# A transformer kernel on one core: transposes moved to the projection banks and row sums moved to VectorE in the cross-attention stages

## The reference

```python
# layer 0: x = x + Attn(LN(x), LN(ctx)) ; x = x + MLP(LN(x))
# layer 1: x = x + SelfAttn(LN(x)) ; x = x + CrossAttn(LN(x), ctx) ; x = x + MLP(LN(x))
xn = layernorm(x, ln1_w, ln1_b)                       # 512 tokens x 512
q = (xn @ Wq).reshape(B, N1, H, hd).transpose(0, 2, 1, 3)   # H = 16 heads of 32
k = kv[:, :, 0].transpose(0, 2, 1, 3)                 # 77 keys for each of the 8 batches
attn = softmax(einsum('bhqd,bhkd->bhqk', q, k) * scale, axis=-1)
o = einsum('bhqk,bhkd->bhqd', attn, v).transpose(0, 2, 1, 3).reshape(B, N1, C1)
x = x + (o @ Wproj + bproj)
```

## Time and profile before

| what | value |
|---|---|
| median of 3 runs | 3474.11 us (3473.83 to 3480.76) |
| the profiled execution's own time | 3480.76 us |
| its span | 3479.0 us |
| PE busy | 3188.6 us, 92% of the span |
| DVE, ACT, POOL busy | 1764.3, 1631.5, 1332.3 us (51, 47, 38%) |
| TensorE's clock as granted, mean | 0.956 of full |
| first cross-attention stage | about 105 to 526 us |
| second cross-attention stage | about 2317 to 2741 us |

### The profile page before, as it was taken

How to read it: one execution, slowest core, us unless ns; L and a number is a source line. 1 busy time by engine, 2 the same in 40 slices (tenths; PEclk the granted TensorE clock), 3 DMA queues, 4 the chain that set the end, 5 groups by cost and what they waited for, 6 DMA issues and landing times. The chain is left out here.

```text
span 3479.0 us, 42311 instructions
## 1 busy us (share of the span) xinstructions
PE 3188.6 (92%) x14480; PEld 2521.0 (72%) x14480; DVE 1764.3 (51%) x2720; ACT 1631.5 (47%) x3492; POOL 1332.3 (38%) x1355
## 2 busy tenths in 40 slices
PE   6599997999999958999999999958999799999999
PEld 5478876888888845666766766636787588888887
DVE  4477754323233225777777777746776442222221
ACT  2376653322222214666666666626777332222222
POOL 0354431333333323666666665644544211111110
PEclk8799998999999978999999999979999899999999
DMA  4422313211111122343343334332222321110000
GB/s 136 119 64 75 88 55 118 70 49 49 49 49 49 49 97 70 92 117 104 101 114 109 103 97 109 99 94 61 82 73 69 106 91 37 37 37 30 30 28 35
DMA packets 215049, 264.36 MB, mean 76 GB/s; under 512 B 78460, under 2 KB 100580, under 8 KB 214836
## 3 DMA queue, kind: packets, MB, share of 16 engines
q1 hardware_dynamic: 214835, 261.66, 25.4%
HBM read 125.12 MB, written 60.42 MB: 53 GB/s over the span
## 5 line engine op out<-in xcount | busy, mean ns | idle before, releaser
L1065 DVE TENSOR_REDUCE L1sa_nmax<-L1sa_s 128x2 f32<-128x1024 f32 x256 | 310.7, 1214 | 213.9 <-PE L1sa_s L884 213.9
L1157 POOL TENSOR_TENSOR L1sa_El<-L1sa_E,L1sa_Eh 128x1024 fp32r<-128x1024 f32 x128 | 320.7, 2506 | 150.4 <-ACT L1sa_Eh L972 131.1
L468 DVE TENSOR_TENSOR L1ff_gl<-L1ff_gf,L1ff_gh 128x512 fp32r<-128x512 f32 x128 | 95.8, 748 | 473.8 <-ACT L1ff_gh L428 473.8
L468 DVE TENSOR_TENSOR L0ff_gl<-L0ff_gf,L0ff_gh 128x512 fp32r<-128x512 f32 x128 | 99.1, 774 | 437.9 <-ACT L0ff_gh L428 437.9
L414 ACT ACTIVATE L1ff_gf<-L1ff_f,cols 128x512 f32<-128x512 f32 x128 | 88.3, 690 | 450.7 <-PE L1ff_f L94 450.7
L414 ACT ACTIVATE L0ff_gf<-L0ff_f,cols 128x512 f32<-128x512 f32 x128 | 88.3, 690 | 450.3 <-PE L0ff_f L94 450.3
L981 ACT ACTIVATE L1sa_E<-L1sa_st 128x1024 f32<-128x1024 f32 x256 | 260.5, 1017 | 48.1 <-PE L1sa_st L896 47.9
L92 PE MATMUL L1ff_f<-L1ff_hTh,L1ff_Wh 128*128 128x512 f32 x512 | 203.3, 397 | 5.7 <-POOL L1ff_hTl L235 5.7
L92 PE MATMUL L0ff_f<-L0ff_hTh,L0ff_Wh 128*128 128x512 f32 x512 | 203.1, 397 | 5.7 <-POOL L0ff_hTl L235 5.7
L972 ACT ACTIVATE L1sa_Eh<-L1sa_E 128x1024 fp32r<-128x1024 f32 x192 | 200.7, 1045 | 0.2
L94 PE MATMUL L1ff_f<-L1ff_hTl,L1ff_Wh 128*128 128x512 f32 x512 | 200.4, 391 | 0.0
(11 more groups left out here) (284 smaller groups left out, 8648.7 us busy)
## 6 DMA issues: line engine op xcount, KB each, us to landing
L1sa_OLN<-L1sa_osb SPq DMA_DIRECT2D x128, 192.0 KB, 2.7
L0ff_xs<-x SPq DMA_DIRECT2D x64, 256.0 KB, 3.0
L1sa_stack_q<-L1sa_parts_q SPq DMA_DIRECT2D x128, 128.0 KB, 2.6
L1sa_stack_k<-L1sa_parts_k SPq DMA_DIRECT2D x128, 128.0 KB, 2.6
L1ff_xs<-x SPq DMA_DIRECT2D x64, 256.0 KB, 3.4
L0ca_xs<-in_x SPq DMA_DIRECT2D x32, 256.0 KB, 3.0
L0ca_stage<-in_x SPq DMA_DIRECT2D x32, 256.0 KB, 2.8
x<-L0ca_stage SPq DMA_DIRECT2D x32, 256.0 KB, 2.0
```

Of the source, the lines that this page charges most:

```text
L468: nc.vector.tensor_tensor(gl[:, j % 2, :], gf[:, j % 2, :], f32(gh[:, j % 2, :]), ALU.subtract)\
L1065: nc.vector.reduce_max(nmax[:, h % 2, 2 * (n % 2):2 * (n % 2) + 2], s_bank[:, :, :], AX.X, negate=True)\
L1157: nc.gpsimd.tensor_tensor(El[:, n % 2, :], E[:, n % 3, :], f32(Eh[:, n % 2, :]), ALU.subtract)\
```

## The change

The `T` transposes become units like `Q` and `O`: they take the `pj` banks in the common turn and stand in `CA_ORDER` behind the last query projection of the batch; their own halves (`T_HALVES`) and their own turn (`turn_bank`) go, and the `t` banks hold probabilities alone. The 36 pieces of a batch (32 before) are dealt out over the 24 halves. DVE sums all tiles, so no exponential has an accumulator. `BIAS` moves to halves 1, 8, 13 and 17. ACT, DVE and POOL take a `T` unit in the half behind the one in which it ends.

```diff
-CA_ORDER = [("Q", 0, 3), ("O", -1, 0), ("O", -1, 1), ("Q", 1, 0), ("O", -1, 2), ("Q", 1, 1), ("O", -1, 3), ("Q", 1, 2)]
-CA_FIRST = [("Q", 0, g) for g in range(3)]
-
-T_HALVES = (3, 4, 5, 6)
+CA_ORDER = ([("Q", 0, 3)] + [("T", 1, c) for c in range(KT)]
+            + [("O", -1, 0), ("Q", 1, 0), ("O", -1, 1), ("Q", 1, 1), ("O", -1, 2), ("O", -1, 3), ("Q", 1, 2)])
+CA_FIRST = [("T", 0, c) for c in range(KT)] + [("Q", 0, g) for g in range(3)]
...
-    quarters = [(*u, c) for u in CA_ORDER for c in range(KT)]
+    quarters = [(*u, c) for u in CA_ORDER for c in range(1 if u[0] == "T" else KT)]
...
-        SUM_BY = ("act", "dve", "act", "dve")
+        SUM_BY = ("dve", "dve", "dve", "dve")
         LAST_TILE = (B - 1, 3 * (TILES - LEAD) // 2)
-        STATS, NORMS, BIAS = (13, 14, 15, 16), (19, 20, 21, 22), (1, 3, 9, 14)
+        STATS, NORMS, BIAS = (13, 14, 15, 16), (19, 20, 21, 22), (1, 8, 13, 17)
...
             def bank_free(u):
                 kind, b, i = units[u - 2]
-                if kind == "Q":
+                if kind == "T":
+                    pe.wait_ge(x.e_hf.sem, x.e_hf.at(b, i))
+                elif kind == "Q":
                     pe.wait_ge(e_ql.sem, e_ql.at(b, i))
...
                 if c == 0 and u >= 2:
                     bank_free(u)
-                if kind == "Q":
+                if kind == "T":
+                    if i == 0:
+                        pe.wait_ge(x.e_xn.sem, x.e_xn.at(b, TT - 1))
+                    ln_transpose(nc, x, bank, i, cst.ident[:, :]).then_inc(x.e_tr.sem, x.e_tr.unit)
+                elif kind == "Q":
...
-                bank = turn_bank("P", b, v)
+                if b * CA_STEPS + v >= 2:
+                    pe.wait_ge(e_pl.sem, e_pl.no(b * CA_STEPS + v - 2))
...
             def evacuate(kind, b, i):
-                if kind == "Q":
+                if kind == "T":
+                    whole(b, i)
+                elif kind == "Q":
                     q_hi(b, i)
...
-                    if half - 1 in T_HALVES and exists(b + 1):
-                        hi(b + 1, T_HALVES.index(half - 1))
...
             def finish(kind, b, i):
-                if kind == "Q":
+                if kind == "T":
+                    hi(b, i)
+                elif kind == "Q":
                     q_lo(b, i)
...
-                    if half - 1 in T_HALVES and exists(b + 1):
-                        lo(b + 1, T_HALVES.index(half - 1))
+                    for kind, n, i in evacs[b * HALVES + half]:
+                        if kind == "T":
+                            lo(n, i)
```

More of the change, by code:

```diff
@@ L1501, in cross_attention @@
         no = {u: i for i, u in enumerate(units)}
[L1504 to L1511, removed]
         def tile_at(half):
@@ L1621, in bank_free @@
                     pe.wait_ge(x.e_res.sem, x.e_res.at(b, i))
[L1623 to L1636, removed]
             def piece(kind, b, i, c):
@@ L1678, in P_transposed @@
                     pe.wait_ge(e_pn.sem, e_pn.at(b, g * TT + TT - 1))
-                bank = turn_bank("P", b, v)
+                if b * CA_STEPS + v >= 2:
+                    pe.wait_ge(e_pl.sem, e_pl.no(b * CA_STEPS + v - 2))
                 for qt in range(TT):
-                    last = nc.tensor.transpose(bank[0:n, qt * P:(qt + 1) * P],
+                    last = nc.tensor.transpose(t_bank[v % 2][0:n, qt * P:(qt + 1) * P],
                                                Pr[:, g, qt, c * P:c * P + n], cst.ident[:, :])
@@ L1695, in _ @@
             cst.wait_ident(pe)
-            for c in range(KT):
-                T(0, c)
-            pe.wait_ge(wt.lo.sem, wt.lo.no(WQ - 1))
             for kind, b, i in CA_FIRST:
-                for c in range(KT):
+                if kind == "Q" and i == 0:
+                    pe.wait_ge(wt.lo.sem, wt.lo.no(WQ - 1))
+                for c in range(1 if kind == "T" else KT):
                     piece(kind, b, i, c)
@@ L1718, in _ @@
                         PV(b - 1, CA_STEPS - 1)
-                    if half in T_HALVES and exists(b + 1):
-                        T(b + 1, T_HALVES.index(half))
             PV(B - 1, CA_STEPS - 1)
@@ L1743, in whole @@
                     act.wait_ge(x.e_hl.sem, x.e_hl.no(n * KT + c - 2))
-                ln_whole(nc, x, t_bank[turn["T", n, c] % 2], c).then_inc(x.e_hf.sem, x.e_hf.unit)
+                ln_whole(nc, x, pj[no["T", n, c] % 2], c).then_inc(x.e_hf.sem, x.e_hf.unit)
             def exp(b, s):
@@ L1762, in p_hi @@
                     act.wait_ge(e_pv.sem, e_pv.no(b * CA_STEPS + v - 2))
-                add_hi(nc, PTh[0:n, v % 2, :], t_bank[turn["P", b, v] % 2][0:n, :], None).then_inc(e_ph.sem, e_ph.unit)
+                add_hi(nc, PTh[0:n, v % 2, :], t_bank[v % 2][0:n, :], None).then_inc(e_ph.sem, e_ph.unit)
             def o_hi(b, g):
@@ L1782, in _ @@
             weights_hi(0, WQ)
-            for c in range(KT):
-                whole(0, c)
             for u in CA_FIRST:
@@ L1798, in _ @@
                         p_hi(b, half // 2)
-                    if half - 1 in T_HALVES and exists(b + 1):
-                        whole(b + 1, T_HALVES.index(half - 1))
                     for u in evacs[b * HALVES + half]:
@@ L1839, in p_lo @@
                 dve.wait_ge(e_ph.sem, e_ph.at(b, v))
-                add_lo(nc, PTl[0:n, v % 2, :], PTh[0:n, v % 2, :], t_bank[turn["P", b, v] % 2][0:n, :], None)\
+                add_lo(nc, PTl[0:n, v % 2, :], PTh[0:n, v % 2, :], t_bank[v % 2][0:n, :], None)\
                     .then_inc(e_pl.sem, e_pl.unit)
@@ L1889, in _ @@
                 normalise(0, t)
-            for c in range(KT):
-                hi(0, c)
             for u in CA_FIRST:
```

## The result

| what | before | after |
|---|---|---|
| median, us | 3473.97 (3473.72 to 3480.76, 4 runs) | 3521.83 (3521.05 to 3522.68, 4 runs) |
| the profiled execution and its span, us | 3480.76, 3479.0 | 3518.35, 3516.6 |
| mean granted clock of TensorE | 0.956 | 0.959 |

The changed kernel is slower by 47.9 us, ratio 1.0133 (95% interval 1.0115 to 1.015). Most of it lies in the two cross-attention stages: from the first load of the stage to the first load of the next one the trace has 422.4 us before and 444.5 after in the first layer, 425.7 and 448.1 in the second, together 44.5 us more. The two profiled executions as wholes differ by less, 37.6 us: the one of the changed kernel was 2.7 to 4.3 us shorter than the four in the table, and outside the two stages its trace is 6.9 us shorter than the one before, at a mean clock of 0.959 against 0.956.

The account below looks back on a forecast made before the run. PE was taken as the bound, busy 92% of the span with no pause in middle batches. Pauses 50.7, clock 24 and row sums 3 made 77.7 us on 3474.1: 3551.8, predicted as 3552, range 3518 to 3584.

Parts of the forecast that it names:

- rival 1: Cross-attention middle batches: the pauses come but the clock holds; 3474.1 + 53.7 = 3528 us, chance 0.20.
- Both pauses: PE waits before the second T (half 3), 1.93 us (second layer 1.99), and the first output projection (half 5), 1.66 us.
- Their number, 14: Seven batches of each layer have a successor, so both pauses occur 14 times, 50.7 us in all.
- The clock, 24 us: Behind the pauses PE's clock falls for 3.5 us, costing 1.7 us, one fully paid a batch: 14 x 1.7 = 24 us.
- Row sums, 3 us: DVE summing all tiles costs 0 in middle batches and +1.5 us per layer in first batches, 3 in all.
- Rivals 2, 3 and 4: Only the first pause, 3505 (0.06); no wait, not slower, 3471 (0.05); DVE delays PE in each batch, 3580 (0.03).
- `BIAS`, SP's loads, the t banks: Moved additions on POOL, 0; earlier loads, 0; t banks free of T, at most 1 us a layer, within the row-sum term.

Follow-up runs that it names:

- e11: The changed kernel with two unread copies added on ACT ahead of the third T's emptying in half 5, lengthening the second pause: 3525.87 us, ratio 1.0155.

## Why the prediction was right in direction and too high in size

The time lies in the stated range, but near its lower end, and not by the forecast's own account. The forecast was both pauses and a clock that falls in most batches, 3535 to 3580 (0.66). What happened is its rival 1, the pauses with a clock that holds, 3528 (0.20), to which the time is within 6 us. The lower end, 3518, does not follow from its words: rival 1 with pauses a tenth shorter is 3474.1 + 45.6 = 3519.7, or 3522.7 with the 3 us of the row sums that rival 1 includes, and by the latter the measured 3521.8 would lie just below it.

*Both pauses.* Right: pauses 1.94 and 1.64 us where the working had 1.93 and 1.66, released by the engines it named. For the second this is in part luck: its chain is 3.28 us and not 3.39, since the maximum starts 0.62 behind the scores (256.18 to 256.80) instead of 0.71, and PE is ready at 1.64 and not 1.73, since the scores take 0.42 there and not 0.50. The two errors cancel.

*Their number, 14.* Too high. The first pause is there 14 times, but the second only 12 times: the first batch of a layer has no batch before it, so no output projection either. Twelve middle batches at 3.6 us give 43 us; with the one fall, 1.6, that is all of the 44.5 us by which the stages grew. In the two first batches the second T waits too, 2.62 and 2.7 us:

```profile
160.10 1.11 PE L221 MATMUL L0ca_pj<-ident,L0ca_xs 128*128 128x128 f32 x4 [2.62 <-DVE L0ca_qTl L105]
```

PE stood idle in that place before the change as well, for 2.8 of 4.1 us, so not all of it is new. The first and the last batches do change, and nearly cancel. The first layer, from the first load to the first scores that PE issues in its second batch, and from those in its last batch to the end of the stage, before and then now:

```profile
104.94:194.51 89.57, 58.18 (x263) 45.71 (x264) 54.47 (x121) 43.69 (x162) 39.68 (x38) 0.77 0.33 92
471.15:527.33 56.18, 49.47 (x226) 37.42 (x224) 25.99 (x55) 21.48 (x79) 17.69 (x20) 0.92 0.18 61
...
103.53:196.90 93.37, 60.66 (x263) 47.96 (x264) 60.02 (x132) 41.20 (x122) 40.05 (x38) 0.74 0.32 88
494.99:548.02 53.03, 46.32 (x226) 35.52 (x224) 27.91 (x60) 19.18 (x59) 17.73 (x20) 1.00 0.19 64
```

The first part is 3.8 us longer, in part by the clock (0.77 and now 0.74), and the last is 3.15 shorter: the same 226 matmuls keep PE busy for 3.15 us less at a clock of 1.00 than at 0.92. In the second layer it is 1.3 us more and 2.1 less (PEclk in the last part 0.92 and now 0.97). So the 50.7 us should have been about 43, and what the first batches added was made up by a higher clock in the last ones, which the prediction had no term for.

*The clock, 24 us.* This is the step that failed: one fall in twelve batches, about 1.6 us (51.33 us from that T to the next, against 49.7). It was argued from two stretches at a stage's start and end, and the two new pauses were added up to 3.6 of 6.5 us as if they were one. The second of these stretches ends in the pause of 1.50 us behind which the clock fell before the change and does not fall now, so it could not show that such a pause brings a fall each time. Two pauses of 1.77 and 1.71 us (e11) gave one fall as well, so their sum does not decide by itself. The price of a fall was right, the number of falls was not. This count is of the profiled execution; the four timed ones ran 2.7 to 4.3 us longer at a mean clock of 0.957 and not 0.959, and no trace says whether they had a fall or two more in these stages. The rule of the Trainium skill, "Perfetto Trace Analysis", Matmul Optimizations, on which the prediction also leaned, holds in kind (longer pauses did lower the clock), but it gives no size, and here it cost next to nothing.

*Row sums, 3 us.* Measured alone as no change (1.0001, which is -3 to +3.5 us by the interval), so the 3 us are neither shown nor excluded.

*Rivals 2, 3 and 4.* Out: both waits are there; PE is idle; and no wait behind `PTl` or on DVE's load appeared in the middle batches, although DVE had 38.0 us to do.

*`BIAS`, SP's loads, the t banks.* No wait that names them appears in the stages' middles. They were not run apart, so their 0 us is read from the waits and not measured.

*What is left.* The stages' growth is 44.5 us and the medians differ by 47.9. The 3.4 us between are less than single executions of the kernel before differ by (3473.7 to 3480.8), and they are not assigned.

## What to carry to other kernels

In a rotation of two buffers what counts is not how many buffers there are but how long the one unit between takes: a unit of 0.44 us cannot cover an emptying whose chain is 2.4 or 3.3 us long, and a short unit that is put into the rotation can open one such gap (here two gaps for four short units). Read the chain from the producer's start to the emptying's end across the other engines' queues, subtract the work between, and the pause is known to about a tenth of a microsecond. A clock penalty is harder: here the same pause of 1.50 us was followed by a fall in one kernel and by none in the other, and of twelve middle batches with a pause of 1.77 us one had a fall. So for pauses of this length a fall in every batch is a bound and not a term of the sum, and the runs give no ground for adding two of them up to one long pause.

## What the runs showed of the hardware

- In one profiled execution of each kernel, pauses of PE of 1.77 idle us were followed by a fall of the granted clock in one middle batch of twelve, of 2.15 to 3.29 in six to ten of twelve and not in the order of their length, of 4.81 in all. A pause of 1.50 us at a stage's end was followed by a fall in one kernel and by none in another.
- DVE's cast to `hTh`, reading and writing SBUF, took 0.44 us on average before and 0.67 now. The long ones run beside POOL's subtraction for the T before: 1.42 us at 260.11, while POOL worked from 259.95 to 261.24. It is off PE's path here.

```profile
259.44 0.43 DVE L231 CAST L0ca_hTh<-L0ca_htmp 128x512 fp32r<-128x512 f32 x1
260.11 1.42 DVE L231 CAST L0ca_hTh<-L0ca_htmp 128x512 fp32r<-128x512 f32 x1 [0.24 <-ACT L0ca_htmp L226]
```

```profile
259.95 1.29 POOL L235 TENSOR_TENSOR L0ca_hTl<-L0ca_htmp,L0ca_hTh 128x512 fp32r<-128x512 f32 x1 [1.00 <-DVE L0ca_hTh L231]
```
